# Attention stage of a two-layer network: another division of the eight PSUM banks, and other engines for two chores

## The reference, cut to what matters

```python
x = _layernorm(x + _L0_attn_ref(x, ...))      # the stage that the change touches
x = _layernorm(x + _L0_ffn_ref(x, ...))       # experts, then a recurrence, then experts again: untouched
...
def _L0_attn_ref(...):                        # 4096 tokens, 16 heads of 16, blocks of 64 tokens
    mid_ctx: block l of the queries looks at blocks l-1, l, l+1 and at the first and the last block
    first_ctx, last_ctx: the first and the last block look at all 64 blocks
    softmax with the row's maximum taken off
```

## Time and profile before

| | us |
|---|---|
| median of 3 runs (lowest, highest) | 1957.84 (1955.69, 1966.75) |
| the profiled execution, its own time | 1955.44 |
| its span | 1953.7 |
| attention's loop of steps (first product of maxima to last values), from the timeline | 128 to 658 |
| attention's tail, to the first instruction of the next stage | 658 to 696 |

### The profile page before, as it was taken

The page is one execution under the profiler, slowest core; times in us unless marked ns, Lnnn a source line. Parts: engine busy times, 40 slices in busy tenths (PEclk is TensorE's granted clock), DMA queues, the critical chain, the costliest instruction groups (busy, mean ns, idle before and its releaser), DMA issues. The chain is left out here.

```text
span 1953.7 us, 35776 instructions
## 1 busy us (share of the span) xinstructions
PE 1691.5 (87%) x12958; PEld 1383.7 (71%) x12958; DVE 1205.7 (62%) x2677; ACT 895.1 (46%) x1805; POOL 619.3 (32%) x571
## 2 busy tenths in 40 slices
PE   5879999999999568879999769889994499999991
PEld 4666666666666447858888635569993499999991
DVE  4566776676667666655555358766665556566543
ACT  2305656666666444443333256544441144444433
POOL 1340000000003645567777424433330212333111
PEclk9889999999999779999999979999997599999996
DMA  5795422443240481024444263001114113333214
GB/s 189 267 168 78 78 52 47 63 78 62 47 62 27 146 273 44 34 62 72 71 74 68 41 151 87 1 1 44 44 44 173 35 34 121 94 95 85 79 15 172
DMA packets 143785, 164.91 MB, mean 84 GB/s; under 512 B 70794, under 2 KB 115968, under 8 KB 143616
## 3 DMA queue, kind: packets, MB, share of 16 engines
q1 hardware_dynamic: 107968, 111.60, 21.5%
q0 software_dynamic: 28544, 47.35, 11.3%
q10 hardware_dynamic: 7104, 3.67, 1.2%
HBM read 104.75 MB, written 61.08 MB: 85 GB/s over the span
## 5 line engine op out<-in xcount | busy, mean ns | idle before, releaser
L772 DVE TENSOR_REDUCE att_neg_max<-att_m_ps 128x1 f32<-128x320 f32 x496 | 230.3, 486 | 123.6 <-PE att_m_ps L519 115.8
L1897 PE MATMUL silu_h_ps<-silu_xT,silu_w_part 128*128 128x320 f32 x1536 | 236.8, 313 | 0.9 <-DVE silu_xT L1993 0.9
L1897 PEld LDWEIGHTS silu_h_ps<-silu_xT,silu_w_part 128*128 128x128 f32 x1536 | 227.3, 189 | 2.1 <-DVE silu_xT L1993 1.3
L519 PE MATMUL att_m_ps<-att_k,att_q 96*128 96x384 f32 x496 | 199.7, 411 | 11.8 <-DMA att_q<-qk 4.2
L905 POOL DMA_DIRECT2D att_q<-att_max_row x40 | 20.2, 505 | 435.8 <-DVE att_max_row L780 435.7
L519 PEld LDWEIGHTS att_m_ps<-att_k,att_q 96*128 96x128 f32 x496 | 94.2, 190 | 72.8 <-DVE att_neg_max L772 29.5
L1862 POOL DMA_INDIRECT summed<-silu_y,all_table x40 | 64.1, 1603 | 256.8 <-DVE silu_y L2033 153.8
L1623 POOL DMA_INDIRECT part<-layer_xT,all_table x72 | 119.3, 1658 | 59.4 <-DVE layer_xT L1744 44.7
L1909 PE MATMUL silu_y_ps<-silu_w_part,silu_h_part 128*128 128x256 f32 x960 | 117.9, 285 | 2.2 <-DVE silu_w_part L2009 2.2
L1909 PEld LDWEIGHTS silu_y_ps<-silu_w_part,silu_h_part 128*128 128x128 f32 x960 | 117.3, 194 | 2.5 <-DVE silu_w_part L2009 2.5
L715 ACT ACTIVATE att_prob_g<-att_g_ps 128x512 f32<-128x512 f32 (+1 forms) x128 | 74.6, 582 | 88.4 <-PE att_g_ps L561 85.3
(11 more groups left out here) (315 smaller groups left out, 4021.6 us busy)
## 6 DMA issues: line engine op xcount, KB each, us to landing
experts_w<-in_dram SPq DMA_DIRECT2D x24, 1024.0 KB, 8.4
qk<-qkv_part POOLq DMA_DIRECT2D x32, 512.0 KB, 3.5
att_k<-qk SPq DMA_DIRECT2D x192, 64.0 KB, 2.3
att_q<-qk SPq DMA_DIRECT2D x168, 64.0 KB, 3.9
v<-qkv_v POOLq DMA_DIRECT2D x8, 544.0 KB, 4.9
att_v<-v SPq DMA_DIRECT2D x8, 544.0 KB, 5.3
qkv_x<-in_dram SPq DMA_DIRECT2D x8, 512.0 KB, 5.6
rows<-att_context SPq DMA_DIRECT2D x8, 512.0 KB, 5.3
```

What stands on the lines that cost most here:

```text
L519: nc.tensor.matmul(bank[:, 0:2 * LOCAL].rearrange("p (a n) -> p a n", a=2), q[b][0:MROW, x, :], local_and_global(b, x), start=True, stop=T ...
L772: ins = nc.vector.tensor_reduce(neg_max[b][:, x - 1:x], bank[:, 0:LOCAL + 2 * BLK], AX.X, ALU.max, negate=True)
L1897: mm = nc.tensor.matmul(h_ps[u % 2][a][:, :], w12_part[f % RING][wp][:, a, k, :], xT[s][xp][:, k, rows], start=(i == 0), stop=(i == 3 * KD ...
```

## The change

Five edits, all in `attend`. (1) Maxima get three banks in place of two, and a unit waits for unit u-3. (2) Scores get one tensor `s_ps` of four banks: in a band step the globals take bank 0 or 1 in turn, and the neighbours take banks 2 and 3 in every step; in full steps the pairs 0,1 and 2,3 alternate. PE waits before the first product into a bank for its last reader. (3) All turned results are kept by ACT, at the head of its step, ahead of the exponential of the globals; DVE keeps none. (4) DVE copies the result of step g-2 first, and reduces all units of the step after that. (5) In the tail POOL normalises nothing; DVE and ACT share the groups, and the last join (`join(DB)`) is the last thing in POOL's queue.

```diff
-        m_ps = [m.ps(f"m_ps{i}", [P, 512]) for i in range(2)]
-        g_ps = m.ps("g_ps", [P, 4, P])
-        b_ps = [m.ps(f"b_ps{i}", [P, 2, 4, P]) for i in range(2)]
+        m_ps = [m.ps(f"m_ps{i}", [P, 512]) for i in range(3)]
+        s_ps = m.ps("s_ps", [P, 4, 4, P])
...
+        def banks_of(i):
+            if i >= DB:
+                return None, slice(2 * (i % 2), 2 * (i % 2) + 2)
+            return i % 2, slice(2, 4)
...
-        NORM_BY = {"dve": (1, 4, 7, 10), "pool": (2, 5, 8, 11, 14), "act": (0, 3, 6, 9, 12, 13, 15, 16)}
+        NORM_BY = {"dve": (1, 3, 5, 7, 9, 11, 13), "act": (0, 2, 4, 6, 8, 10, 12, 14, 15, 16)}
...
-                if u >= 2:
-                    pe.wait_ge(m_reduced, u - 1)
+                if u >= 3:
+                    pe.wait_ge(m_reduced, u - 2)
...
+            def bank_read(bank):
+                if bank in readers:
+                    pe.wait_ge(*readers[bank])
...
+                bank_read(order[third])
                 if third == 0:
...
-                    if g > 0:
-                        pe.wait_ge(g_exp, e * DB + i)
...
+                    readers[own] = g_exp, e * DB + i + 1
                 elif third == 1:
-                    if g >= 2:
-                        pe.wait_ge(exp_done, g - 1)
...
                     mm.then_inc(s_done, 1)
+                    for bank in order[1:]:
+                        readers[bank] = exp_done, g + 1
...
             for g in range(TOTAL):
+                x = g % 2
+                if finished(g - 3) is not None:
                     act.wait_ge(pv_done, g - 1)
                     act.wait_ge(o_out, results(g - 2))
-                    keep(act, nc.scalar.copy, w)
+                    keep(finished(g - 3))
...
-                    keep_even(g)
...
             for g in range(TOTAL):
-                for at in units[:1]:
-                    maximum(*ms, at)
                 out(g - 2)
-                w = finished(g - 3)
-                if w is not None and w % 2 == 1:
-                    dve.wait_ge(pv_done, g - 1)
-                    keep(dve, nc.vector.tensor_copy, w)
-                for at in units[1:]:
+                for at in units:
                     maximum(*ms, at)
```

More of the change, by code:

```diff
@@ L302, in attend, with written @@
         block = ctx.enter_context(nc.Block())
+        def banks_of(i):
+            if i >= DB:
+                return None, slice(2 * (i % 2), 2 * (i % 2) + 2)
+            return i % 2, slice(2, 4)
+        def written(i):
+            own, two = banks_of(i)
+            return ([] if own is None else [own]) + list(range(4))[two]
         def blocks_of(n):
@@ L536, in scores @@
                 b = e % 2
-                both = b_ps[i % 2][:, :, :, :]
+                own, two = banks_of(i)
+                both = s_ps[:, two, :, :]
+                order = written(i)
                 if i >= DB:
                     s = i - DB
-                    if third == 0:
-                        if s == 0:
-                            row_there(e, PARTS - 1)
-                        pe.wait_ge(exp_done, g - 1)
-                    flat = both.rearrange("p a l t -> p (a l t)")
+                    if third == 0 and s == 0:
+                        row_there(e, PARTS - 1)
                     for j in ((0,), (1, 2), (3,))[third]:
-                        mm = nc.tensor.matmul(flat[:, 2 * j * P:2 * (j + 1) * P], keys(b, 8 * s + 2 * j),
+                        if j % 2 == 0:
+                            bank_read(order[j // 2])
+                        mm = nc.tensor.matmul(both[:, j // 2, 2 * (j % 2):2 * (j % 2) + 2, :], keys(b, 8 * s + 2 * j),
                                               q[b][0:ROWS, 0:NBLK:NBLK - 1, :], start=True, stop=True)
@@ L550, in scores @@
                         mm.then_inc(s_done, 1)
+                        for bank in order:
+                            readers[bank] = exp_done, g + 1
                     return
                 l0, nb = 1 + 4 * i, blocks_of(i)
+                bank_read(order[third])
                 if third == 0:
@@ L676, in _, with keep @@
             act.wait_ge(probs_cleared, 1)
+            def keep(w):
+                e, n = divmod(w, OUTS)
+                tiles = slice(ENDS, ENDS + 2) if n == DB else tiles_of(n)
+                act.wait_ge(out_turned, w + 1)
+                turned = o_ps[:, (1 + w % 2) * P:(2 + w % 2) * P].rearrange("p (n a d) -> p n a d", n=2, a=2)
+                nc.scalar.copy(context[:, tiles, e:H:PAIRS, :], turned[:, 0:tiles.stop - tiles.start, :, 0:VW]).then_inc(kept, 1)
             def roots(first, stop):
@@ L742, in _ @@
             normalise(16)
-            for n in (11, 13, 15):
-                copy_rows(act, nc.scalar.copy, n)
+            copy_rows(act, nc.scalar.copy, 15)
         @block.vector
@@ L923, in join @@
                     nc.gpsimd.tensor_tensor(rows[:, t, :], scaled[t % 2][:, :], hidden[n % 2][:, j, :], ALU.add).then_inc(added, 1)
-            def normalise(n):
-                pool.wait_ge(shift_done, max(n - FIRST_ROOTS + 2, 1))
-                tiles = tiles_of(n)
-                for t in range(tiles.start, tiles.stop):
-                    ins = nc.gpsimd.tensor_scalar(rows[:, t, :], rows[:, t, :], mean_var[:, t, 0:1], inv[:, t:t + 1],
-                                                  ALU.subtract, ALU.mult)
-                ins.then_inc(normed["pool"], 1)
             for b in range(2):
```

99 lines of the change are left out of this document (47 added, 52 removed).

## The result

The changed kernel took 1906.6 us (median of 4 runs, 1904.19 to 1908.86), the kernel before 1959.12 us in the runs beside it (1955.69 to 1966.75): ratio 0.973, 95% interval 0.969 to 0.976. It is faster, by 2.7%. The profiled execution took 1908.86 us with a span of 1907.1, against 1953.7 before: 46.6 less, where the prediction had 47.5.

The account below looks back on a forecast made before the run. Two maxima banks tie PE and DVE together, so neither fills a step. Seven pairs 44.5, last pair 1.0 and tail 2.0 make 47.5 us off the profiled 1955.44: 1907.9, put at 1910 for the median; range 1896 to 1922.

Parts of the forecast that it names:

- Full steps, the third bank: Steps 16 to 23 of a pair: with three maxima banks 16.7 us against 20.26, 3.6 less per pair.
- Band loop: Band steps: handoff 0.15, bare weight load 0.10, 0.90 to the exponentials, 1.38 of exponentials; 2.53 us, above PE's 2.42.
- the signs that the prediction named: Profile after: pairs 56 to 58 us apart, full steps 1.95 to 2.05, band steps 2.45 to 2.55 with PE awaiting ACT.
- What the one pair of score banks costs: Band steps: 0.11 us above PE's own work, in some eleven steps of eight pairs, 10 us in all.
- Keeps: ACT's keep at the step's head: covered, so no cost; the turn's wait of 0.11 us goes in half the steps.
- Step 11's "t": Step 11's opening maxima product waits for two small reductions behind DVE's copy: 0.65 us (0.3 to 1.0), step 2.45.
- Last pair: Last pair of heads, start to last maxima product: 28.6 us against 29.55, 1.0 less; POOL's joins cover its full steps.
- Tail: After the loop, ACT and DVE normalise instead of POOL: 2 us gained, between 0 and 4.7, nothing if transfers bind.
- scores giving back the gain: Rival, chance 0.21: band steps stay near 2.65 us, full steps still gain; 28 us off, 1930.
- The copy falling behind the reductions: Rival, chance 0.05, slower: DVE's late copy delays ACT's keep and exponentials in band steps; 1988 us.
- That nothing changes: Rival, chance 0.08: PE is full at 98% busy, stalls only move; 1956 to 1958 us.
- The third rival: Chance 0.05: DVE's copy waits for a step's whole reductions, band step 3.3 us; 62 lost, 30 gained, 1988 us.

Follow-up runs that it names:

- the run with two banks: The changed kernel with two banks for the maxima instead of three, all else as changed: 1946.64 us, ratio 0.994 to the kernel before.
- the reordered run: The changed kernel with the third maxima product ahead of the first band score product in band steps: 1896.8 us, ratio 0.969 to the kernel before.
- the run with the banks alone: The changed kernel with banks and tail as changed, but keeps shared by ScalarE and VectorE as before: 1931.9 us, ratio 0.986 to the kernel before.

## Why the prediction was right, point by point

**The total** (1910 predicted, 1906.6 measured, in the range) came as near as it did partly by luck: its terms were off to both sides. The last pair starts 50.0 us earlier (599.35 to 549.31), where seven pairs were to give 44.5; from there to the last copy 2.1 are gained where 1.0 was predicted, and the tail loses 0.4 where it was to gain 2.0. So attention's end came 51.7 us earlier (695.81 to 644.10), where the terms summed to 47.5. That the profiled spans differ by 46.6 only is chance: the untouched stages behind took 1263.0 us in the one execution and 1257.9 in the other, 5.1 more, within their scatter over the thirteen, so it is no effect of the change that these runs show. The medians, which don't hang on one execution, differ by 52.5 (1959.12 to 1906.6).

**Full steps, the third bank**: right. 16.7 predicted, 16.65 measured; the run with two banks shows that 3.3 of the 3.6 to 3.8 us are the bank's. TensorE's own work was taken as 1.95 and a step takes 1.96.

**Band loop**: the mechanism was right and shown (what ScalarE takes longer, the step takes longer), a term was mis-sized. "Handoff 0.15 + bare weight load 0.10" measured 0.05 + 0.05. I had taken the row nearest in kind and kept 0.05 as the low end; it was the low end. The 0.90 measured 0.96, the exponentials 1.38 as said: 2.44, not 2.53. That is the greater part of the difference in steps 0 to 7 and 12 to 15 (0.5 and 0.3 a pair). Of the signs that the prediction named, the waits came, and four of the full steps at 1.96; pairs of 56 to 58 and band steps of 2.45 to 2.55, all alike, did not quite: pairs take 55.75, and steps 3 to 7 2.39 to 2.45, with 2.80 and 2.60 in steps 1 and 2.

**What the one pair of score banks costs**: 0.11 a step by the prediction. The step is 0.07 above TensorE's own work, which the reordered run shows to be 2.37 (2.42 predicted). The Trainium skill (Perfetto Trace Analysis, section Matmuls) asks to rotate banks: rightly, and yet here rotating three banks under the maxima was worth 5.9 us a pair, and two pairs under the scores 0.2 while the maxima had two. Since the loop could be shortened by order alone, the only wait left for it in pairs 1 to 6 of the reordered kernel is 0.27 us, once a pair. Three banks for maxima together with two pairs for the neighbours' scores would make nine with the globals' and the results' banks, so no run shows that.

**Keeps**: the step that was weakest. It counted the turn's wait (0.11 in half the steps) and held the rest to be covered. Alone the keeps are worth 1.6 us a pair, and on top of the bank 3.6. The sum came out near, because each step had been costed as free of both stalls at once; its shares (0.20 for the bank in every band step, whatever the keeps do) are not what each part brings alone. What it lacked is the question that the run with the banks alone answers: once the unit's stall is gone, which wait is late next? It is the turn's, for the keep, of ScalarE in one step and of VectorE in the next.

**Step 11's "t"**: right, 0.65 predicted, 0.55 on TensorE's row, and steps 10 and 11 together 4.92 against 2.5 + 2.45.

**Last pair**: 1.0 predicted. Its last "t" comes 28.00 us behind its start (549.31 to 577.31), 1.55 less than the earlier trace rows, against 0.95. Up to the last result's copy the pair is 2.1 shorter, the rest being in the steps under POOL's chain.

**Tail**: wrong. I took 2 us, between 0 and 4.7; it measured -0.4. The prediction had named the case ("bound by what the transfers move, nothing is gained") and the number for it, 16 x 1.42 us, and then chose near the middle. The rate in the stretches of the kernel before (333 to 344 GB/s in four of five) spoke for it beforehand.

**The rivals**: scores giving back the gain did not happen, with the loop at 2.44. The copy falling behind the reductions did not either: the keep of the step shown above starts at 336.68, as the exponentials end. That nothing changes was ruled out by the full steps. (The third rival's 1988 starts from the profiled execution; 62 lost and 30 gained on the median's 1957.84 would be 1990.)

## What to carry to other kernels

When two stalls sit in one step of an engine's queue, price each with the other gone. Taking away one alone may only lengthen the other, and then the two edits are worth more together (7.3 us a pair) than apart (3.8 + 1.6). Where a buffer is single, read the loop through it (release, work of the producer, work of the consumer), and ask which of the producer's instructions in it could stand ahead of the wait: moving one of 0.24 us took 1.2 us off each pair here. These are the prices of this kernel, not a rule. And before costing a tail by who computes what, divide its bytes by the rate that the stretches of the trace show.

## What the runs showed that I had not expected

From the end of ScalarE's exponential to the start of TensorE's weight load 0.05 us pass, and 0.05 more to the product. In the earlier trace rows 0.15 pass to the product behind a longer exponential.

Instructions of ScalarE on 128x256 values last 0.38 us each, but two in a row take 0.66, and four of 128x128 0.79 where one of 128x512 takes 0.60: an instruction more costs 0.06 us in a row of its kind. A mean duration is no price.

VectorE's 128x26 operation at the tail's start took 0.60 us while a POOL addition ran, in the changed kernel:

```profile
614.79 0.76 POOL L923 TENSOR_TENSOR att_context<-att_context 128x272 f32<-128x272 f32 x1 [1.95 <-ACT att_context L691]
...
614.99 0.60 DVE L841 SCALAR_TENSOR_TENSOR att_shift<-att_mean_var,att_inv 128x26 f32<-128x26 f32 x1
```

In the kernel before, with no POOL work at that moment, it took 0.19. In the run with the banks alone, whose tail is otherwise the changed kernel's, POOL's addition ended at 641.86 and the operation, from 642.13, took 0.19 too. So it goes with the overlap in these traces, but no run varied that alone, and the cause is open.
